# Loads four blocks ahead in a graph kernel's gate stage, dense rows two groups ahead in its mean stage

## The chip, the cores and the metric

One core of a Trainium2 chip. The metric is the device time of one execution in microseconds. A block below is 512 edges (4 tiles of 128); a node group is 1024 nodes. There are 98 of each.

## What is computed

Four graph layers over 100,000 nodes with 64 features and 50,000 edges sorted by destination: a mean of neighbours, a residual gated convolution (two gates), a four-head attention and a weighted SAGE layer, each followed by `x = layernorm(x + layer(x))`. What matters here is the end of the first layer, the dense half of the second layer that needs no edges, and the second layer's first gate:

```python
h = x + L0(x)                       # mean of neighbours, then layernorm -> x1
# first gate, per edge (src, dst), weights folded:
gate = sigmoid(k[dst] + q[src])     # k, q, v = x1 @ Wk1, x1 @ Wq1, x1 @ Wv1
agg  = segment_sum(gate * v[src], dst)
h1   = relu((agg + x1 @ Ws1 + b1) @ Wl1 + bl1)
# nodes without edges take the dense path: two matrix products, relu, add, layernorm
```

## The kernel before

The program is a row of stages; a barrier of all engines stands between two of them. Each stage writes an in-order program for each engine by hand; engines meet by counting semaphores alone. `over_pairs` calls a body `step(n, i, s, ...)` for every block, two to a loop iteration; `s = n % 2` picks one of two buffers. `ahead(n, i, s, k)` names block n+k, and `fresh(n)` is true where no earlier user of the buffer exists.

**Mean stage** (`spread_mean`, tag mb). GpSimd scatters the rows of runs (`x1_run`) into the table `x1_tab`: four indirect DMAs to a block (L1555), after indices that ScalarE copies (L1094). Beside it runs the dense path of node group n (`NodeStage`): SyncE loads `mb_xn` (L1533); TensorE transposes it (turn, L1131); ScalarE copies it (L1140); TensorE multiplies (hide, L1665); ScalarE takes the relu (L1619); TensorE multiplies again (multiply, L1149) into one PSUM bank; VectorE adds in four passes and a tiny one (`n_add`, L1573 to L1582); ScalarE squares (L1625); VectorE reduces (L1587); ScalarE takes the root (L1629, L1633); VectorE scales (`n_scale`, L1593); SyncE stores (L1159). A small edge MLP rides along, one half in even and the other in odd steps: in an odd step ScalarE runs z, abs, exp, ln (L1785 to L1793), VectorE `soft` (L1756), TensorE its second product (L1821). A load of rows n+2 waits until `n_add` of n has read its buffer (semaphore `n_used`, sent at L1577). In step n, ScalarE and TensorE turn and multiply group n+1, and VectorE reduces and scales n, then adds n+1.

**Gate stage** (`first_gate`, tag ga). Blocks go from last to first. For each: SyncE loads the block's own rows (`near`, L1860) and the flags that say which edges share a destination (`same`, 128 partitions, L1866); ScalarE copies the own rows into `ends` (put_near, L1975); GpSimd gathers the source rows with four indirect DMAs (L1102) after their indices (L1968); TensorE transposes (turn, L2026); ScalarE copies the lower half (L1989), VectorE scans the upper half by the flags (`spread_near`, L1915); TensorE forms the gates (produce, L2034); ScalarE takes the sigmoid (L1995); VectorE multiplies (L1922) and scans (`add_up`, L1931); TensorE mixes (L2042); VectorE finishes (L1939, L1944); SyncE stores (L1875). The order in step n is

```python
# SyncE:    load_near(n+2), load_same(n+2), store(n)
# ScalarE:  copy(n+2), locate(n+2), open_gate(n+2), index(n+4), put_near(n+4)
# TensorE:  mix(n), turn(n+2), produce(n+2)
# VectorE:  spread_near(n+2), weigh(n+1), add_up(n+1), finish(n)
# GpSimd:   rows_of(n+2)
```

`turn`, `spread_near`, `copy` and `produce` of a block reuse the buffers of the block two before: `spread_near(n)` waits for `mix(n-2)`, `rows_of(n)` for `turn(n-2)`.

Of the kernel before, what the change touches and what calls it, by code (L numbers as in the profile page):

```python
# [5 lines left out]
P = 128  # L6
D = 64
# [1494 lines left out]
def spread_mean(nc, a, st):  # L1502
# [3 lines left out]
    with Phase(nc, "mb") as ph:  # L1506
# [11 lines left out]
        node_turn, node_hidden, node_out = bank[0:3]  # L1518

        @block.sync  # L1520
        def _(sp):
            def load(n, i, s):
                if not fresh(n):
                    sp.wait_ge(scattered[s], 64 * i)
                    hold(sp, ph.passed)
                sp.dma_start(flat(run[s][:]), st["x1_run"][bass.ds(n * P, P)]).then_inc(run_in[s], 16)

            def load_x(n, i, s):
                if not fresh(n):
                    sp.wait_ge(node.turned, n - 1)  # L1530
                    sp.wait_ge(n_used, n - 1)
                    hold(sp, ph.passed)
                sp.dma_start(flat(xn[s][:]), table_rows(st["x1_node"], first_node(st, n))).then_inc(x_in[s], 16)  # L1533

            def step(n, i, s, first, last):
                if there(n + 2, BLOCKS):
                    load_x(*ahead(n, i, s, 2))
                    load(*ahead(n, i, s, 2))
                node.store(sp, st["attn_x"], n, i, s)

            for s in (0, 1):
                load(s, 0, s)
                load_x(s, 0, s)
            mlp.load(sp)
            over_pairs(sp, BLOCKS, step)
            node.all_stored(sp)
# [18 lines left out]
        def _(dve):  # L1565
            steps_n = Steps(dve, n_chain, 2)

            def n_add(n, i, s):
# [4 lines left out]
                nc.vector.tensor_tensor(node.v[s][:], product_rows(node_out), over_rows(rows[:, st["B_MIX2"], :]),  # L1573
# [22 lines left out]
            def step(n, i, s, first, last):  # L1596
                n_reduce(n)
                mlp.vector_before(dve, i, s, first)
                mlp.vector(dve, i, s, first)
                n_scale(n, i, s)  # L1600
                if there(n + 1, BLOCKS):
                    n_add(*ahead(n, i, s, 1))

            n_add(0, 0, 0)
            over_pairs(dve, BLOCKS, step)
            mlp.last_keep(dve)

        @block.scalar
        def _(act):
# [41 lines left out]
            node.copy(act, 0, node_turn)  # L1651
            n_relu(0)
            n_squares(0, 0, 0)
            over_pairs(act, BLOCKS, step)

        @block.tensor
        def _(pe):
# [10 lines left out]
            def n_multiply(n):  # L1668
                node.multiply(pe, n, node_out, st["w_pair"][2][:], h_t, softened)

            def step(n, i, s, first, last):
                more = there(n + 1, BLOCKS)
                if more:
                    n_turn(*ahead(n, i, s, 1))
                mlp.tensor_before(pe, i, s, first)
                if more:
                    n_hide(n + 1)
                mlp.tensor_after(pe, i, s, first)
                if more:
                    n_multiply(n + 1)  # L1680

            n_turn(0, 0, 0)
            n_hide(0)
            n_multiply(0)
# [144 lines left out]
def first_gate(nc, st):  # L1829
# [3 lines left out]
    with Phase(nc, "ga") as ph:  # L1833
# [11 lines left out]
        gathered, near_in, same_in, stored = ([ph.sem(f"{n}{s}") for s in (0, 1)] for n in (  # L1845
            "gathered", "near_in", "same_in", "stored"))
# [8 lines left out]
        def _(sp):  # L1855
# [13 lines left out]
            def step(n, i, s, first, last):  # L1869
                if there(n + 2, BLOCKS):  # L1870
                    load_near(*ahead(n, i, s, 2))
                    load_same(*ahead(n, i, s, 2))
# [4 lines left out]
            for s in (0, 1):  # L1877
                load_near(s, 0, s)
                load_same(s, 0, s)
            over_pairs(sp, BLOCKS, step)  # L1880
# [22 lines left out]
        def _(dve):  # L1903
            steps = Steps(dve, chain, 1)

            def spread_near(n, i, s):

                dve.wait_ge(turned, n + 1)
                dve.wait_ge(same_in[s], 16 * (i + 1))
# [15 lines left out]
            def add_up(n, i, s):  # L1925

                dve.wait_ge(paid, n + 1)
                if not fresh(n, 1):
                    dve.wait_ge(carried, n)
# [34 lines left out]
        def _(act):  # L1964
# [50 lines left out]
            over_pairs(act, BLOCKS, step)  # L2015

        @block.tensor
        def _(pe):
# [1643 lines left out]
```

## Time and profile before

| | us |
|---|---|
| median of 3 executions | 11201.8 (11200.99 to 11210.53) |
| the profiled execution: its time | 11221.07 |
| its span (first to last instruction) | 11219.4 |
| mean stage, in that span | 2447.7 to 3593.5 |
| gate stage | 3593.5 to 4928 |
| busy over the span: TensorE, VectorE, ScalarE, GpSimd | 49%, 58%, 39%, 61% |

The profile is of one execution. Times in its rows count from the start of the span. A timeline row gives start, duration, engine, line and operation (several instructions merged, with "xcount"), output<-input, and in brackets how long the engine had been idle and what ended that. PE is TensorE's matmul, PEld its weight load, DVE VectorE, ACT ScalarE, POOL GpSimd, SPq SyncE's queue. PEclk is the TensorE clock granted, as a share of full speed.

### The profile page before, as it was taken

How to read it: one execution, taken by the hardware profiler on the slowest of the kernel's cores; microseconds unless marked ns; L12 is line 12 of the kernel's file. 1: busy time of each engine (PE TensorE's matmuls, PEld its weight loads, DVE VectorE, ACT ScalarE, POOL GpSimd, SP SyncE). 2: the span in 40 equal slices, each digit the busy share in tenths (PEclk: the TensorE clock that was granted, in tenths of full speed). 3: DMA queues.
4: the chain of work that ended last, by engine and by line, in shares of the span. 5: the costliest groups of instructions: out<-in, count | busy, mean ns of one | idle time of the engine just before them, and what ended most of it. 6: DMA issues, size and time to landing. Idle time of an engine off the chain costs nothing. (4 is left out here: it accounts for less than half of the span.)

```text
span 11219.4 us, 129468 instructions
## 1 busy us (share of the span) xinstructions
PE 5525.8 (49%) x23165; PEld 4503.1 (40%) x23165; DVE 6495.9 (58%) x15506; ACT 4356.2 (39%) x11357; POOL 6848.6 (61%) x6784
## 2 busy tenths in 40 slices
PE   4210056655554333335555677677666666663222
PEld 1000055543333222223334666666666655553222
DVE  6767655544443333347776666666699974443333
ACT  1668644433332111137774333333355543331111
POOL 1767577753333222247777777777655557777777
PEclk6555577765555566655555555555566656665555
DMA  3000044441222111122221111111133334443222
GB/s 121 8 21 7 22 145 149 151 123 62 65 67 62 48 48 49 48 57 68 71 71 38 27 27 27 27 27 27 52 98 99 99 99 137 135 135 87 61 61 51
DMA packets 589304, 780.08 MB, mean 70 GB/s; under 512 B 153140, under 2 KB 306811, under 8 KB 585819
## 3 DMA queue, kind: packets, MB, share of 16 engines
q1 hardware_dynamic: 388540, 599.31, 16.5%
q0 software_dynamic: 200704, 180.15, 7.8%
q8 instruction: 17, 0.28, 0.0%
q14 instruction: 43, 0.34, 0.0%
HBM read 468.37 MB, written 322.23 MB: 70 GB/s over the span
## 5 line engine op out<-in xcount | busy, mean ns | idle before, releaser
L2603 DVE CUSTOM_DVE_ANT_0 att_junk<-bank,att_away 128x512 f32<-128x512 f32 x1568 | 973.5, 686 | 120.0 <-PE bank L2766 105.3
L1102 POOL DMA_INDIRECT ga_ends<-x_tab,ga_src_i x392 | 382.1, 975 | 950.7 <-ACT ga_src_i L1968 854.6
L1555 POOL DMA_INDIRECT x_tab<-mb_run,mb_put_i x392 | 389.9, 995 | 735.2 <-ACT mb_put_i L1094 621.1
L1003 PE MATMUL bank<-att_payload,att_match 128*128 128x68 f32 x3136 | 620.8, 383 | 190.9 <-DVE att_payload L2619 96.4
L1003 PEld LDWEIGHTS bank<-att_payload,att_match 128*128 128x128 f32 x3136 | 609.6, 298 | 221.5 <-issue 221.5
L2034 PE MATMUL bank<-ga_ends_t,w_gate 128*128 128x512 f32 x196 | 202.3, 1135 | 890.3 <-ACT ga_ends_t L1989 890.3
L1915 DVE TENSOR_TENSOR_SCAN ga_ends_t<-ga_same,ga_ends_t,bank 64x512 f32<-64x512 f32 x97 | 123.4, 1272 | 853.7 <-PE bank L2026 853.7
L471 POOL DMA_INDIRECT half_sorted<-ka_out_row,ka_put_i x392 | 397.1, 1013 | 286.6 <-ACT ka_put_i L604 172.1
L1102 POOL DMA_INDIRECT gb_ends<-h_tab,gb_src_i x392 | 432.0, 1102 | 150.1 <-issue 118.5
L674 POOL DMA_INDIRECT edges<-kb_out_row,kb_put_i x392 | 423.3, 1080 | 154.2 <-issue 121.9
L1102 POOL DMA_INDIRECT sa_ends<-x_tab,sa_dst_i x392 | 398.2, 1016 | 153.6 <-issue 135.5
L1102 POOL DMA_INDIRECT att_ends<-attn_x,att_dst_i x392 | 397.6, 1014 | 131.3 <-issue 102.1
L3605 PE MATMUL bank<-ident,sb_pay 128*65 128x128 f32 x392 | 109.5, 434 | 747.1 <-DVE sb_pay L3492 747.1
L1102 POOL DMA_INDIRECT ma_ends<-in_x,ma_src_i x392 | 376.6, 961 | 158.8 <-issue 130.8
L3460 POOL DMA_INDIRECT out<-sb_out,sb_put_i x392 | 397.6, 1014 | 121.7 <-issue 119.3
L2554 POOL DMA_INDIRECT attn_tab<-att_new,att_put_i x392 | 386.7, 986 | 135.9 <-issue 124.7
L1102 POOL DMA_INDIRECT sb_ends<-h_tab,sb_src_i x392 | 379.4, 968 | 137.6 <-issue 118.9
L2130 POOL DMA_INDIRECT attn_x<-gb_out,gb_put_i x392 | 387.6, 989 | 123.1 <-issue 105.2
L1102 POOL DMA_INDIRECT sa_ends<-x_tab,sa_src_i x392 | 379.4, 968 | 119.4 <-issue 110.6
L1102 POOL DMA_INDIRECT att_state<-attn_tab,att_row_i x392 | 370.4, 945 | 123.0 <-issue 123.0
L1102 POOL DMA_INDIRECT ma_ends<-in_x,ma_dst_i x392 | 370.2, 945 | 119.5 <-issue 111.2
L1102 POOL DMA_INDIRECT att_ends<-attn_x,att_src_i x392 | 370.0, 944 | 119.5 <-issue 116.1
(515 smaller groups left out, 20349.6 us busy)
## 6 DMA issues: line engine op xcount, KB each, us to landing
da_agg<-attn_tab SPq DMA_DIRECT2D x98, 288.0 KB, 2.9
attn_tab<-ka_attn_start SPq DMA_DIRECT2D x24, 1152.0 KB, 29.7
x_tab<-ma_wide SPq DMA_DIRECT2D x98, 260.0 KB, 2.0
ma_xn<-in_x SPq DMA_DIRECT2D x98, 256.0 KB, 3.4
x_node<-ma_n_out SPq DMA_DIRECT2D x98, 256.0 KB, 2.1
h_tab<-ma_n_out SPq DMA_DIRECT2D x98, 256.0 KB, 2.1
mb_xn<-x_node SPq DMA_DIRECT2D x98, 256.0 KB
attn_x<-mb_n_out SPq DMA_DIRECT2D x98, 256.0 KB, 2.1
```

The source lines that it names most:

```text
L471: nc.gpsimd.indirect_dma_start(st["half_sorted"], bass.IndirectOffsetOnAxis(ap=put_i[s][:, q:q + 1], axis=0), out_row[s][:, q, :], None).t ...
L674: nc.gpsimd.indirect_dma_start(st["edges"], bass.IndirectOffsetOnAxis(ap=put_i[s][:, q:q + 1], axis=0), out_row[s][:, q, :], None).then_in ...
L1003: ins = self.nc.tensor.matmul(bank[:, u * w:(u + 1) * w], self.match[s][:, t, u * P:(u + 1) * P], self.payload[s][:, t, :], start=(t == 0) ...
L1102: nc.gpsimd.indirect_dma_start(dst, None, table, bass.IndirectOffsetOnAxis(ap=index[:, q:q + 1], axis=0)).then_inc(sem, 16)
L1555: nc.gpsimd.indirect_dma_start(st["x1_tab"], bass.IndirectOffsetOnAxis(ap=put_i[s][:, q:q + 1], axis=0), run[s][:, q, :], None, bounds_che ...
L1915: nc.vector.tensor_tensor_scan(ends_t[s][0:D, ::-1], same[s][0:D, ::-1], turn_b[s][0:D, ::-1], before, ALU.mult, ALU.add).then_inc(spread, 1)
L2034: nc.tensor.matmul(gate_b[s][:], st["w_gate"][0][:], ends_t[s][:], start=True, stop=True).then_inc(produced, 1)
L2130: nc.gpsimd.indirect_dma_start(st["attn_x"], bass.IndirectOffsetOnAxis(ap=put_i[s][:, q:q + 1], axis=0), out[s][:, q, :], None, bounds_che ...
L2554: nc.gpsimd.indirect_dma_start(st["attn_tab"], bass.IndirectOffsetOnAxis(ap=put_i[s][:, q:q + 1], axis=0), new[s][:, q, :], None, bounds_c ...
L2603: ins = nc.vector.tensor_tensor_reduce(junk[h % 2][:, q, :], logit_t[h % 2][:], away[s][:, q, :], 1.0, -2.0 * BIG, ALU.subtract, ALU.max, ...
L3460: nc.gpsimd.indirect_dma_start(dest, bass.IndirectOffsetOnAxis(ap=put_i[s][:, q:q + 1], axis=0), out[s][:, q, :], None, bounds_check=N - 1 ...
L3605: ins = nc.tensor.transpose(turn_b[s][0:K, q * P:(q + 1) * P], pay[s][:, q, :], ident[:])
```

## The change

Mean stage: every part of the dense path moves one step earlier than VectorE: turn, hide and multiply of group n+2 run in step n; the last product alternates between two PSUM banks; VectorE scales group n-1, adds n+1, reduces n; ScalarE takes the root of n-1; SyncE stores n-1 after its loads. Gate stage: SyncE loads own rows of block n+4 in step n; the flags load is split into its upper half (64 partitions, for `spread_near`, block n+4) and its lower half (for `add_up`, block n+2), with a semaphore each; the store is that of n-1; TensorE's order is mix(n), produce(n+2), turn(n+3).

```diff
@@ spread_mean, sync
                     load_x(*ahead(n, i, s, 2))
                     load(*ahead(n, i, s, 2))
-                node.store(sp, st["attn_x"], n, i, s)
+                if not fresh(n, 1):
+                    node.store(sp, st["attn_x"], n - 1, i + s - 1, 1 - s)
@@ vector
             def step(n, i, s, first, last):
-                n_reduce(n)
                 mlp.vector_before(dve, i, s, first)
                 mlp.vector(dve, i, s, first)
-                n_scale(n, i, s)
+                if not fresh(n, 1):
+                    n_scale(n - 1, i + s - 1, 1 - s)
                 if there(n + 1, BLOCKS):
                     n_add(*ahead(n, i, s, 1))
+                n_reduce(n)
@@ scalar
-                more = there(n + 1, BLOCKS)
-                if more:
-                    node.copy(act, n + 1, node_turn)
-                n_root(n)
-                if more:
-                    n_relu(n + 1)
-                if there(n + 2, BLOCKS):
+                further = there(n + 2, BLOCKS)
+                if not fresh(n, 1):
+                    n_root(n - 1)
+                if further:
+                    node.copy(act, n + 2, node_turn)
                     index(*ahead(n, i, s, 2))
                 mlp.scalar(act, i, s, first)
-                if more:
+                if further:
+                    n_relu(n + 2)
+                if there(n + 1, BLOCKS):
                     n_squares(*ahead(n, i, s, 1))
@@ tensor
-            def n_multiply(n):
-                node.multiply(pe, n, node_out, st["w_pair"][2][:], h_t, softened)
+            def n_multiply(n, s):
+                pe.wait_ge(softened, n + 1)
+                if not fresh(n):
+                    pe.wait_ge(node.added, n - 1)
+                for r in range(4):
+                    ins = nc.tensor.matmul(node_out[s][:, r * P:(r + 1) * P], h_t[:, r * P:(r + 1) * P],
+                                           st["w_pair"][2][:], start=True, stop=True)
+                ins.then_inc(node.done, 1)
+
+            def step(n, i, s, first, last):
+                further = there(n + 2, BLOCKS)
+                if further:
+                    n_turn(*ahead(n, i, s, 2))
                 mlp.tensor_before(pe, i, s, first)
+                if further:
+                    n_hide(n + 2)
                 mlp.tensor_after(pe, i, s, first)
+                if further:
+                    n_multiply(n + 2, s)
...
@@ first_gate, sync
+            def load_near_same(n, i, s):
+                if not fresh(n):
+                    sp.wait_ge(spread, n - 1)
+                    hold(sp, ph.passed)
+                sp.dma_start(same[s][0:D, :], st["same_next"][bass.ds(back(n), 1)].broadcast_to([D, BLOCK])
+                             ).then_inc(near_same_in[s], 16)
...
-                sp.dma_start(same[s][:], st["same_next"][bass.ds(back(n), 1)].broadcast_to([P, BLOCK])
+                sp.dma_start(same[s][D:P, :], st["same_next"][bass.ds(back(n), 1)].broadcast_to([D, BLOCK])
                              ).then_inc(same_in[s], 16)
...
+            def step(n, i, s, first, last):
+                if there(n + 4, BLOCKS):
+                    load_near(*ahead(n, i, s, 4))
+                if there(n + 2, BLOCKS):
+                    load_same(*ahead(n, i, s, 2))
+                if there(n + 4, BLOCKS):
+                    load_near_same(*ahead(n, i, s, 4))
+                if not fresh(n, 1):
+                    store(n - 1, i + s - 1, 1 - s)
...
@@ tensor
                 mix(n, i, s)
                 if there(n + 2, BLOCKS):
-                    turn(*ahead(n, i, s, 2))
                     produce(*ahead(n, i, s, 2))
+                if there(n + 3, BLOCKS):
+                    turn(*ahead(n, i, s, 3))
 
             turn(0, 0, 0)
             turn(1, 0, 1)
             produce(0, 0, 0)
+            turn(2, 1, 0)
             produce(1, 0, 1)
```

Four blocks of own rows and flags are loaded ahead of the loop, and two node groups are turned and multiplied ahead of the loop of the mean stage.

## Rows read from the trace of the kernel before

**Rows 1.** Windows: length, busy us (x) of PE, PEld, DVE, ACT, POOL; PEclk, DMA share, GB/s

```profile
3000.00:3300.00 300.00, 151.19 (x481) 102.26 (x481) 122.34 (x220) 91.37 (x247) 103.08 (x104) 0.57 0.21 66
...
4200.00:4500.00 300.00, 94.12 (x308) 66.19 (x308) 93.41 (x132) 44.27 (x110) 86.42 (x88) 0.63 0.19 48
...
7000.00:7500.00 500.00, 352.57 (x1584) 324.09 (x1584) 348.76 (x1133) 182.81 (x471) 380.13 (x394) 0.58 0.13 27
```

**Rows 2.** Waits, 3650 to 4850 us: total us, times, longest

```profile
ACT ga_ends L1975 <- DMA ga_near<-x_run: 850.0, 88, 10.0
```

**Rows 3.** Timeline of the gate stage, two blocks

```profile
4200.99 0.42 ACT L1975 ACTIVATE ga_ends<-ga_near 128x256 f32<-128x256 f32 x1 [9.56 <-DMA ga_near<-x_run]
...
4202.09 2.08 PE L2034 MATMUL bank<-ga_ends_t,w_gate 128*128 128x512 f32 x2 [9.33 <-ACT ga_ends_t L1989]
...
4204.81 0.20 ACT L1968 ACTIVATE ga_src_i<-src_g 128x4 int32 x1
...
4206.42 1.27 DVE L1915 TENSOR_TENSOR_SCAN ga_ends_t<-ga_same,ga_ends_t,bank 64x512 f32<-64x512 f32 x1 [8.54 <-PE bank L2026]
...
4209.67 0.94 POOL L1102 DMA_INDIRECT ga_ends<-x_tab,ga_src_i  x1 [0.30 <-issue]
...
4210.74 0.43 DVE L1944 SCALAR_TENSOR_TENSOR ga_out<-ga_v,is_head 128x256 f32<-128x256 f32 x1 [0.37 <-DVE ga_v L1939]
4211.48 0.36 SPq L1875 DMA_DIRECT2D h_tab<-ga_out  x1
4212.59 0.34 SPq L1860 DMA_DIRECT2D ga_near<-x_run  x1
...
4214.72 0.42 ACT L1975 ACTIVATE ga_ends<-ga_near 128x256 f32<-128x256 f32 x1 [9.70 <-DMA ga_near<-x_run]
...
4228.30 0.42 ACT L1975 ACTIVATE ga_ends<-ga_near 128x256 f32<-128x256 f32 x1 [9.57 <-DMA ga_near<-x_run]
```

**Rows 4.** Tile view of ga_ends: the gathers' time from issue to landing

```profile
DMA to landing us min/median/max: 2.3/2.5/4.1
```

**Rows 5.** Timeline of the second gate: turn and mix back to back

```profile
5309.84 1.08 PE L2312 MATMUL bank<-ident,gb_ends 128*128 128x128 f32 x4 [5.86 <-DMA gb_ends<-h_tab,gb_src_i]
...
5310.72 1.80 PE L2329 MATMUL bank<-w_mix,gb_ends_t 128*128 128x64 f32 x8
```

**Rows 6.** Timeline of the mean stage, one pair of steps

```profile
3004.98 0.69 DVE L1577 SCALAR_TENSOR_TENSOR mb_n_v<-mb_n_v,mb_xn 128x512 f32<-128x512 f32 x1
...
3005.91 0.33 SPq L1533 DMA_DIRECT2D mb_xn<-x_node  x1
...
3011.35 0.20 ACT L1094 ACTIVATE mb_put_i<-tail_put 128x4 int32 x1
...
3013.87 0.68 DVE L1593 TENSOR_TENSOR mb_n_out<-mb_n_v,mb_rstd 128x512 f32<-128x512 f32 x1
3014.01 0.93 PEld L1821 LDWEIGHTS bank<-mb_mlp_w,mb_mlp_soft 128*128 128x128 f32 x4 [4.86 <-DVE mb_mlp_soft L1756]
...
3015.03 1.91 PE L1149 MATMUL bank<-w_pair,mb_h_t 128*128 128x128 f32 x8
...
3016.74 1.06 PE L1131 MATMUL bank<-ident,mb_xn 128*128 128x128 f32 x4
...
3028.99 0.33 SPq L1533 DMA_DIRECT2D mb_xn<-x_node  x1
```

**Rows 7.** Timeline of the mean stage's start

```profile
2448.10 0.43 SPq L1533 DMA_DIRECT2D mb_xn<-x_node  x1
...
2450.85 1.09 PE L1131 MATMUL bank<-ident,mb_xn 128*128 128x128 f32 x4 [9.06 <-DMA mb_xn<-x_node]
...
2452.62 2.08 PE L1665 MATMUL bank<-mb_n_rows_t,w_pair 128*128 128x512 f32 x2 [0.69 <-ACT mb_n_rows_t L1140]
```

**Rows 8.** Tile view of mb_put_i: the scatters' time from issue to landing

```profile
DMA to landing us min/median/max: 2.1/2.2/14.0
```

**Rows 9.** Timeline of the gate stage's start: one gate product

```profile
3610.48 1.12 PE L2034 MATMUL bank<-ga_ends_t,w_gate 128*128 128x512 f32 x2 [1.83 <-ACT ga_ends_t L1989]
```

More of the change, by code:

```diff
@@ L1517, in spread_mean @@
         block = ph.ctx.enter_context(nc.Block())
-        node_turn, node_hidden, node_out = bank[0:3]
+        node_turn, node_hidden, node_out = bank[0], bank[1], bank[2:4]
         @block.sync
@@ L1545, in _ @@
             over_pairs(sp, BLOCKS, step)
+            node.store(sp, st["attn_x"], BLOCKS - 1, BLOCKS // 2 - 1, 1)
             node.all_stored(sp)
@@ L1572, in n_add @@
                     dve.wait_ge(node.finished, n - 1)
-                nc.vector.tensor_tensor(node.v[s][:], product_rows(node_out), over_rows(rows[:, st["B_MIX2"], :]),
+                nc.vector.tensor_tensor(node.v[s][:], product_rows(node_out[s]), over_rows(rows[:, st["B_MIX2"], :]),
                                         ALU.add).then_inc(node.added, 1)
@@ L1650, in _ @@
                 index(s, 0, s)
-            node.copy(act, 0, node_turn)
-            n_relu(0)
+            for s in (0, 1):
+                node.copy(act, s, node_turn)
+                n_relu(s)
             n_squares(0, 0, 0)
             over_pairs(act, BLOCKS, step)
+            n_root(BLOCKS - 1)
         @block.tensor
@@ L1666, in n_hide @@
                                  ).then_inc(hidden, 1)
-            def n_multiply(n):
-                node.multiply(pe, n, node_out, st["w_pair"][2][:], h_t, softened)
+            def n_multiply(n, s):
[6 more added lines that the diff above has]
+                ins.then_inc(node.done, 1)
             def step(n, i, s, first, last):
-                more = there(n + 1, BLOCKS)
-                if more:
-                    n_turn(*ahead(n, i, s, 1))
+                further = there(n + 2, BLOCKS)
+                if further:
+                    n_turn(*ahead(n, i, s, 2))
                 mlp.tensor_before(pe, i, s, first)
-                if more:
-                    n_hide(n + 1)
+                if further:
+                    n_hide(n + 2)
                 mlp.tensor_after(pe, i, s, first)
[L1679 to L1684, printed above, removed]
+                if further:
+                    n_multiply(n + 2, s)
+            for s in (0, 1):
+                n_turn(s, 0, s)
+                n_hide(s)
+                n_multiply(s, s)
             over_pairs(pe, BLOCKS, step)
@@ L1844, in first_gate @@
                           "finished chain")
-        gathered, near_in, same_in, stored = ([ph.sem(f"{n}{s}") for s in (0, 1)] for n in (
-            "gathered", "near_in", "same_in", "stored"))
+        gathered, near_in, near_same_in, same_in, stored = ([ph.sem(f"{n}{s}") for s in (0, 1)] for n in (
+            "gathered", "near_in", "near_same_in", "same_in", "stored"))
         block = ph.ctx.enter_context(nc.Block())
@@ L1865, in load_same, with store @@
                     hold(sp, ph.passed)
-                sp.dma_start(same[s][:], st["same_next"][bass.ds(back(n), 1)].broadcast_to([P, BLOCK])
+                sp.dma_start(same[s][D:P, :], st["same_next"][bass.ds(back(n), 1)].broadcast_to([D, BLOCK])
                              ).then_inc(same_in[s], 16)
[L1869 to L1872, printed above, removed]
+            def store(n, i, s):
                 sp.wait_ge(finished, n + 1)
@@ L1875, in step @@
                 sp.dma_start(run_rows(st["h1_tab"], back(n)), flat(out[s][:])).then_inc(stored[s], 16)
[L1877 to L1880, printed above, removed]
+            def step(n, i, s, first, last):
[7 more added lines that the diff above has]
+                    store(n - 1, i + s - 1, 1 - s)
+            for n in range(4):
+                load_near(n, n // 2, n % 2)
+                load_near_same(n, n // 2, n % 2)
+                if n < 2:
+                    load_same(n, 0, n)
+            over_pairs(sp, BLOCKS, step, tail=6)
+            store(BLOCKS - 1, BLOCKS // 2 - 1, 1)
             for s in (0, 1):
@@ L1908, in spread_near @@
                 dve.wait_ge(turned, n + 1)
-                dve.wait_ge(same_in[s], 16 * (i + 1))
+                dve.wait_ge(near_same_in[s], 16 * (i + 1))
                 if not fresh(n, 1):
@@ L1927, in add_up @@
                 dve.wait_ge(paid, n + 1)
+                dve.wait_ge(same_in[s], 16 * (i + 1))
                 if not fresh(n, 1):
@@ L2014, in _ @@
                 put_near(s + 2, 1, s)
-            over_pairs(act, BLOCKS, step)
+            over_pairs(act, BLOCKS, step, tail=6)
         @block.tensor
```

1 line of the change is left out of this document (added).

## The prediction, made before the changed kernel was run

> **What bounds the kernel now.** The engines' shares of the whole span say little, since a dozen stages with different limits stand in a row; the change touches two. I read first the windows view by stage [rows 1]: in the mean stage the busiest engine, TensorE, works 151.19 of 300 us, in the gate stage 94.12 of 300 (VectorE 93.41, GpSimd 86.42). No engine is full and the DMA engines are at 0.19 to 0.21, so both stages are bound by a ring of waits, not by work. Two stages of 1146 and 1334 us hold what can be won.
>
> **Gate stage.** The waits view names the ring: ScalarE waits 850.0 us for the own rows (`near`) in 88 blocks [rows 2]. The timeline shows it once round [rows 3]. VectorE's finish of block n ends at 4211.17; SyncE first stores, and only then issues the load of block n+3 (4212.59); the rows are there at 4214.72; put_near stands ahead of `copy(n+2)` in ScalarE's queue, so the gate product, the mix and the turn all wait behind it. From 4200.99 to 4228.30 are two blocks: **13.66 us a block**.
>
> **Mean stage.** The load of node rows n+2 is issued when n_add has read its buffer (4.98 + 0.69, issue at 3005.91), and turn, copy, hide, relu, multiply and add of a group follow each other almost within one step. One load to the one two steps later takes 28.99 − 5.91 = **23.08 us a pair of steps** [rows 6], 11.54 a step.
>
> **The change in the gate stage.** Removed: the near load from that ring. In step n it now loads n+4. In SyncE's queue it stands behind the upper flags of n+3 (which wait for the scan of n+1) and behind the store of n−2; both are released at least one block before ScalarE wants the rows in step n, and a load takes 2.13 us (4212.59 to 4214.72), so it is covered by more than half a block. Its cost on the path is 0 and it would cost up to its 2.13 a block if that cover went. Added: one more DMA on SyncE. The queue has four a block instead of three; a store and the issue behind it take 4212.59 − 4211.17 = 1.42 together with the wake-up, so four take under 5.7 us even at that price each, less than the period below. The lower flags wait for `add_up(n)`; behind them stand the upper flags and the store, which only VectorE's finish of two blocks on and the next stage want. Cost 0; without that cover 1.42 a block.
>
> What is late next is the gather. Its indices still stand behind the sigmoid of `open_gate(n+2)`, and so behind the product of n+2, and `turn(n+4)` now comes just behind the product of n+3. Between two products of the same buffer, produce(n+2) and produce(n+4), lie these steps in series:
>
> - product end (2.09 + 2.08 = 4204.17) to the index copy at 4204.81: 0.64
> - index to the issue of the fourth gather, 4204.81 to 4209.67: 4.86 [rows 3]
> - issue to landing: 2.5 [rows 4]
> - turn(n+4) and mix(n+2) back to back, 5309.84 to 5312.52: 2.7 with the first weight load [rows 5]
> - spread_near(n+4), which may not start before mix(n+2) has read its buffer: 1.27 and about 0.04 to start
> - the product: 2.08 and 0.05
>
> The sum is 14.14 for two blocks, **7.07 a block**. The rings beside it are shorter. One block of TensorE alone (turn and mix 2.7, scan 1.31, product 2.13) is 6.14. GpSimd's four issues are (4209.67 − 4204.81) + 0.94, under 5.8. On VectorE scan, product, second scan and finish run from 4206.42 to 4211.17, that is 4.75. The gain is 13.66 − 7.07 = 6.59 a block. I count it for 94 of 98 blocks (the first sets up, the last three already have no loads to wait for): 619 us. Against it stands the start, where `turn(2)` is now queued ahead of `produce(1)` and must wait for the third gather: by the steps above the first finish comes some 5 us later, an estimate. **Net −614.**
>
> The bounds: the landing can be 2.3 to 4.1 [rows 4]. At 4.1 for every block the ring is 15.7, or 7.9 a block; with TensorE at the higher clock (below) it is 6.1.
>
> **The change in the mean stage.** Nothing is added but a second PSUM bank. The moves take the reduce, root and scale of n and the product of n+1 off the series path, since VectorE adds n+1 from a product made one step earlier. What is left in series over two steps, from the index copy of an odd step, is [rows 6, 7]:
>
> - index, z, abs, exp, ln, soft and scale, 3011.35 to 3014.55: 3.20
> - two passes of n_add until the buffer is free: twice 0.69 and gaps, 1.52
> - SyncE's issue after that, 3005.67 to 3005.91: 0.24
> - the load: 2.75 (2448.10 to 2450.85, the same load with three others beside it)
> - turn 1.09, copy until the next product starts 0.68, hide 2.08
> - the MLP's first product and multiply; the like pair runs from 3014.01 to 3016.94: 2.93
> - the next turn up to 3017.80: 0.86; its copy until the index: 0.55
>
> The sum is **15.9 a pair**. VectorE's and ScalarE's ring is shorter: an even step is three full passes and a reduce more (each 0.69), a root and a scale, some 5.6, and an odd one has the 3.2 of the MLP on top, about 14.5 together. The stores now stand behind the loads in SyncE's queue; the load in the sum waits for `n_used`, which comes after `finished` of the group before, so that queueing costs 0. The scatters have 15.9 us for their eight issues, which take 8 × 1.28 (the 0.97 to 1.0 of one and 0.3 between) = 10.2; cover enough. The gain is 23.08 − 15.9 = 7.18 a pair, for 47 of 49 pairs: **−337**. The load is the term I know least: no row shows its landing in the middle of the stage. It lies between 2.1 (a like load of half the size in the gate stage) and, if it meets the scatters, about the gathers' longest 4.1; that is −0.65 to +1.35 a pair.
>
> **The sum.** 614 + 337 = 951 us off the profiled execution's 11221.07 gives 10270. That execution was 19.3 us above the median of the runs, so on the median's scale I forecast **10251**.
>
> **Where a rule and the rows part.** At 3610.48 one gate product took 1.12 us, at 4202.09 it took 2.08 [rows 3, 9]: the higher and the lower of TensorE's two levels, 2.4 and 1.2 GHz. TensorE today rests 9.33 us ahead of each gate product; after the change its longest rest in a block is about 1.4. I keep 2.08, because in the stage at 7000 us TensorE is busy 352.57 of 500 us, as densely as the changed gate stage would be (4.8 of 7.07), and is granted 0.58 [rows 1].
> The Trainium skill (TensorE: Matmul & The Clock Gate, "HAM oscillation") speaks the other way: long idle gaps are what sends the clock back, so closing them should keep it released. By that rule the sum would be that of rival A; the row at 7000 does not agree with it.
>
> **Rivals.**
> *A, the clock stays up* (chance 0.08). A product saves 0.96, the mix and turn together about 0.9 by the same ratio: 1.9 in the gate ring, 6.1 a block, 90 us more. In the mean stage hide, the product pair and two turns save some 2.6 a pair, 122 more. The time is 10040. For it: the short gaps. Against: 0.58 at 7000.
> *B, transfers collide* (0.14). At half the period the same bytes give DMA shares of 0.3 to 0.4, in bursts, and every gather and load lands late: gathers at 4.1, 0.8 a block more, 78 us; the node load at 4.1, 63 us more; and some 40 more (an estimate) where GpSimd issues each gather slower. The time is about 10430.
> *C, own rows or another SyncE wait still end last in the gate stage* (0.05), because SyncE's queue has four waits in order. Then only the mean stage gains: 11202 − 337 = 10865. Against it speaks that every wait in that queue is satisfied a block early.
> *D, slower* (0.03): broadcast loads clog the DMA engines. At the start of the mean stage, where eight small broadcast loads go out, a scatter took 14.0 us to land instead of 2.2 [rows 8]. The flags are such loads, and there are now two to a block. If each gather landed after 14.0, the gate ring would be 14.14 + 11.5 = 25.6, or 12.8 a block, 81 us faster than today; if the node load in the mean stage, which now ends last there, took 14 too, its pair would be 15.9 − 2.75 + 14 = 27.2, 192 us slower. The time would be 11202 + 111 = 11313. It turns at a landing of about 13 us in both. Against it: today's flags land without delaying a gather, 2.5 in the median.
> The Trainium skill (DMA: Bandwidth & Descriptors, "Rules for kernel authors") says two transfers to disjoint partition halves serialize and are not worth issuing; no row here shows a split flags load. Both halves have a block or more of slack, so this alone only feeds D.
>
> **How the numbers follow.** My forecast has 0.70. Its own range: the gate ring 6.9 to 8.0 a block, the mean pair 14.9 to 18, gives 10160 to 10440. The range that holds 8 in 10 is a little wider, 10130 to 10460: A and C to D stay out, B is in. Same means within 0.2% (22 us), about what a measurement of this kernel can tell; a landing just there needs a mix of C and D: 0.02. Faster 0.95, slower 0.03.
>
> **What would show it.** In the changed profile: the gate stage about 720 us long; the wait of put_near for `ga_near` gone, and in its place TensorE's turn waiting for the gathers and VectorE's scan waiting for the mix; GpSimd waiting for the index copy about 2 us a block; blocks in pairs of about 6.1 and 7.9 us. In the mean stage a pair of steps of 15.9, with TensorE waiting about 2.4 us in even steps for `mb_xn`, and no wait of VectorE for L1149's product. Products of 2.08 say the clock stayed; 1.12 says A. All other stages keep their lengths. The forecast is wrong if the gate block is over 8 us, or if a pair of the mean stage stays above 18.

## The result and the profile after

The changed kernel takes **10282.77 us** in the median (10278.6 to 10287.13, 4 runs) against 11202.19 of the kernel before beside it: ratio 0.9178 [0.9162, 0.9194]. The prediction was 10251, with 10130 to 10460. Below, a stage's length is the time from its first load to the next stage's first load, in the profiled execution.

| us | before | after | predicted step |
|---|---|---|---|
| mean stage | 1145.8 | 784.9 (−361) | −337 |
| gate stage | 1334.4 | 780.2 (−554) | −614 |
| second gate (code unchanged) | 1080.8 | 1063.2 | 0 |
| profiled execution | 11221.07 | 10278.6 (−942.5) | −951 |

The windows view of the kernel after, one row in the mean stage and one in the gate stage (length; busy us of PE, PEld, DVE, ACT, POOL; PEclk; DMA share; GB/s), answers [rows 1]:

```profile
2500.00:3200.00 700.00, 417.71 (x1654) 283.15 (x1653) 422.48 (x763) 311.33 (x855) 374.97 (x359) 0.78 0.31 97
3300.00:3950.00 650.00, 364.99 (x1176) 250.20 (x1176) 356.37 (x503) 159.81 (x420) 326.52 (x336) 0.55 0.35 85
```

No engine is full in either stage (60% at most): rings of waits still set the time, only shorter ones. TensorE's granted clock rose from 0.57 to 0.78 in the mean stage; in the gate stage it went from 0.63 to 0.55 [rows 1]. Such a mean also covers the time in which TensorE rests: the gate products themselves took 2.0 us or more in nearly every block before, and 1.10 in 22 of 98 after.

**Gate stage.** The waits view after, 3350 to 3900 us, about 71 blocks (waiting instruction, releaser, total us, times, longest):

```profile
DVE ga_ends_t L1945 <- PE bank L2073: 205.2, 71, 5.4
ACT ga_gate L2026 <- PE bank L2065: 170.1, 69, 2.7
...
POOL ga_ends L1102 <- PE bank L2057: 149.0, 29, 5.9
PE bank L2057 <- DMA ga_ends<-x_tab,ga_src_i: 128.0, 36, 5.1
...
POOL ga_ends L1102 <- ACT ga_src_i L1999: 52.3, 33, 4.9
```

The 850 us of [rows 2] are gone (put_near waits 4.2 us in the whole stage). In their place stand the waits that the prediction named: the scan for the mix, the turn for the gathers, GpSimd for the indices. (The view puts 149.0 us of GpSimd's waits down to a turn, L2057. By the program the gathers wait only for the turn of two blocks before, which is long done then; the turn named ends within 0.01 us of the index copy, 3602.35 + 1.06 and 3603.21 + 0.20, so the index copy is the release.) The timeline of the kernel after follows the ring once round (start, duration, engine, line, operation):

```profile
3600.51 2.04 PE L2065 MATMUL bank<-ga_ends_t,w_gate 128*128 128x512 f32 x2 [1.51 <-ACT ga_ends_t L2020]
...
3603.21 0.20 ACT L1999 ACTIVATE ga_src_i<-src_g 128x4 int32 x1
...
3606.07 1.10 PE L2065 MATMUL bank<-ga_ends_t,w_gate 128*128 128x512 f32 x2 [1.41 <-ACT ga_ends_t L2020]
...
3607.86 0.34 SPq L1873 DMA_DIRECT2D ga_near<-x_run  x1
...
3608.07 0.94 POOL L1102 DMA_INDIRECT ga_ends<-x_tab,ga_src_i  x1 [0.30 <-ACT ga_src_i L1999]
...
3608.54 0.50 SPq L1886 DMA_DIRECT2D ga_same<-same_next  x1
...
3611.53 1.09 PE L2057 MATMUL bank<-ident,ga_ends 128*128 128x128 f32 x4 [4.37 <-DMA ga_ends<-x_tab,ga_src_i]
...
3612.41 1.80 PE L2073 MATMUL bank<-w_mix,ga_ends_t 128*128 128x64 f32 x8
...
3614.35 1.27 DVE L1945 TENSOR_TENSOR_SCAN ga_ends_t<-ga_same,ga_ends_t,bank 64x512 f32<-64x512 f32 x1 [4.67 <-PE bank L2073]
...
3615.72 2.04 PE L2065 MATMUL bank<-ga_ends_t,w_gate 128*128 128x512 f32 x2 [1.51 <-ACT ga_ends_t L2020]
```

Product end to index 0.66 (3602.55 to 3603.21), index to fourth issue 4.86, issue to turn 3.46, turn to mix end 2.68, scan and wake-up 1.51, product 2.04: 15.21 for two blocks, against 14.14 in the prediction. The blocks come as 5.56 and 9.65. Over the stage a pair takes 15.47 (90 loads of L1873, so 89 blocks, from 3276.5 to 3964.9); in the pairs on either side of the one shown the last gather is used 3.73 and 3.74 after its issue (3592.59 to 3596.32 and 3623.27 to 3627.01).

**Mean stage.** The waits view after, 2600 to 3200 us (39 pairs of steps), then a line of the same view before, 2600 to 3500 us, that has no counterpart after, and then the timeline of one pair after:

```profile
ACT mb_square L1629 <- DVE mb_var L1589: 206.1, 77, 4.7
...
DVE mb_mlp_soft L1769 <- ACT mb_mlp_e L1806: 176.8, 39, 5.0
...
PE bank L1131 <- DMA mb_xn<-x_node: 137.1, 48, 4.0
```

```profile
DVE mb_n_v L1573 <- PE bank L1149: 266.2, 78, 4.5
```

```profile
2811.95 0.33 SPq L1533 DMA_DIRECT2D mb_xn<-x_node  x1
...
2815.05 0.63 PE L1131 MATMUL bank<-ident,mb_xn 128*128 128x128 f32 x4 [3.91 <-DMA mb_xn<-x_node]
...
2816.44 2.07 PE L1671 MATMUL bank<-mb_n_rows_t,w_pair 128*128 128x512 f32 x2 [0.66 <-ACT mb_n_rows_t L1140]
...
2821.23 1.06 PE L1131 MATMUL bank<-ident,mb_xn 128*128 128x128 f32 x4
...
2822.82 0.20 ACT L1094 ACTIVATE mb_put_i<-tail_put 128x4 int32 x1
...
2822.98 1.13 PE L1671 MATMUL bank<-mb_n_rows_t,w_pair 128*128 128x512 f32 x2 [0.69 <-ACT mb_n_rows_t L1140]
...
2825.34 0.68 DVE L1595 TENSOR_TENSOR mb_n_out<-mb_n_v,mb_rstd 128x512 f32<-128x512 f32 x1
...
2826.96 0.69 DVE L1579 SCALAR_TENSOR_TENSOR mb_n_v<-mb_n_v,mb_xn 128x512 f32<-128x512 f32 x1
...
2827.89 0.33 SPq L1533 DMA_DIRECT2D mb_xn<-x_node  x1
```

From load to load 15.94 (23.08 in [rows 6]; predicted 15.9; over the stage a pair takes 15.6, by the loads at 2484.30 and 3202.27, 46 pairs apart): load to turn 3.10, turn and copy 1.39, hide to the end of the next turn 5.85, copy to index 0.53, index to the end of scale 3.20, two adds and the issue 1.87. TensorE waits for the load in about every even step, and VectorE no longer waits for the last product.

### The profile page after: what moved, and what is told of

Read it like the earlier page. It is cut to its first block and busy times, and to the rows that moved or that the text cites. A ratio compares the mean times of both kernels' runs of the same rounds, so it can differ in the third digit from the quotient of the medians.

```text
span 10276.9 us, 130260 instructions
## 1 busy us (share of the span) xinstructions
PE 5401.1 (53%) x23165; PEld 4394.1 (43%) x23165; DVE 6499.3 (63%) x15506; ACT 4347.1 (42%) x11357; POOL 6834.7 (67%) x6784
## 5 line engine op out<-in xcount | busy, mean ns | idle before, releaser
L1557 POOL DMA_INDIRECT x_tab<-mb_run,mb_put_i x392 | 410.8, 1048 | 358.2 <-ACT mb_put_i L1094 248.5
L2921 POOL TENSOR_TENSOR da_weighed<-da_v,rows 128x512 f32<-128x512 f32 x98 | 124.6, 1271 | 414.7 <-DVE da_v L2985 414.7
L3638 PEld LDWEIGHTS bank<-ident,sb_pay 128*65 128x65 f32 x392 | 70.5, 220 | 766.3 <-DVE sb_pay L3525 766.3
```

Of the source, the lines that this page charges most:

```text
L1557: nc.gpsimd.indirect_dma_start(st["x1_tab"], bass.IndirectOffsetOnAxis(ap=put_i[s][:, q:q + 1], axis=0), run[s][:, q, :], None, bounds_che ...
L2921: nc.gpsimd.tensor_tensor(weighed[s][:], v[s][:], over_rows(rows[:, st["B_LNG"], :]), ALU.mult).then_inc(weighing, 1)
L3638: ins = nc.tensor.transpose(turn_b[s][0:K, q * P:(q + 1) * P], pay[s][:, q, :], ident[:])
```

## The experiments

The first eight runs (`mean_only` to `store_only`, then `no_flags` to `store_index`) were made on one chip, where the kernel before took 11217.36 (first four) and 11206.28 us (next four). `no_loads` and the three with early indices at the end came last. These last four ran on **another chip, where the kernel before took 12811.52 us** (12796.39 to 12842.88). There they are compared with each other and by ratio; against the first chip only with the caution that the second gate, unchanged, takes 1325 to 1327 us there instead of 1063 to 1086. The traces show where: there ScalarE waits 217.3 us in 47 waits (L1060, `no_loads`) for something that the profile calls "remote", of which the traces of the first chip show none. In the first gate's stage three of the four show no such wait either, and `turn_two_index_first` 14.4 us. The mean stage, the same code in all of them, takes 791 to 804 us there instead of 785. What "remote" stands for here is open.

### One stage alone

`mean_only` is the kernel before with the new `spread_mean`; `gate_only` the kernel before with the new `first_gate`.

> The change in the mean stage alone, the gate stage as before. Theory 1 (the two stages gain apart, their gains add): the mean stage takes 785 us as in the changed kernel, the gate stage 1334 as before, the time 11202 - 361 = about 10840. Rival (some of the gate's gain comes from what the mean stage leaves behind, such as a warmer clock or warmer queues, or the reverse): mean stage over 800 us, or a gate stage that is not 1334, and gains that do not add up to 919.

> The change in the gate stage alone. Theory 1: mean stage 1146 us, gate stage 780, the time about 11202 - 555 = 10647. Rival: as for the run before it. If theory 1 holds, the two gains add to 919 within 15 us.

Measured: 10850.81 (0.9676 [0.966, 0.9692]) and 10643.25 (0.949 [0.9475, 0.9506]); the mean stage 782.9 in the one, the gate stage 777.8 in the other, as in the whole. The gains of 3.24% and 5.10% make 8.34% against 8.22% together, which is within the intervals. (In us it is 941 against 919, more than the 15 allowed for beforehand; the kernel before was itself 15 us slower in this round.) With the stages' lengths this makes the two halves independent, and each may be explained by itself. The waits of `gate_only` are those of the whole (the turn for the gathers 144.0 us in 43 times from 3700 to 4300).

### Indices ahead of the sigmoid

```diff
@@ first_gate, scalar, step (and likewise ahead of the loop)
                     locate(*ahead(n, i, s, 2))
+                    if there(n + 4, BLOCKS):
+                        index(*ahead(n, i, s, 4))
                     open_gate(*ahead(n, i, s, 2))
                 if there(n + 4, BLOCKS):
-                    index(*ahead(n, i, s, 4))
                     put_near(*ahead(n, i, s, 4))
```

> The changed kernel, but ScalarE copies the gather's indices of block n+4 before the sigmoid of n+2, so that the gathers no longer wait for the product. Theory 1 (the gate ring is product, sigmoid, index, four gathers and their landing, turn, mix, scan, product: 15.2 to 15.5 us for two blocks): the ring breaks there and what is left is TensorE's own ring of turn, mix, scan and product, 6.1 to 6.5 us a block; gate stage 620 to 660 us instead of 780, time 10140 to 10170. Rival 2 (the scan's wait for the mix, or GpSimd's own issue rate with a store and four loads beside it, is what ends last): gate stage within 20 us of 780, time 10260 to 10290.

Measured: **10094.37** (0.9001 [0.8986, 0.9016]), gate stage 586.0: faster than expected, and the best version of all. Timeline of this run, and one line of its waits view (3350 to 3850 us, 77 blocks):

```profile
3600.00 0.19 ACT L1999 ACTIVATE ga_src_i<-src_g 128x4 int32 x1
...
3600.65 2.05 PE L2066 MATMUL bank<-ga_ends_t,w_gate 128*128 128x512 f32 x2 [1.41 <-ACT ga_ends_t L2020]
...
3605.07 0.94 POOL L1102 DMA_INDIRECT ga_ends<-x_tab,ga_src_i  x1 [0.30 <-issue]
...
3606.66 2.04 PE L2066 MATMUL bank<-ga_ends_t,w_gate 128*128 128x512 f32 x2 [1.51 <-ACT ga_ends_t L2020]
...
3608.49 1.06 PE L2058 MATMUL bank<-ident,ga_ends 128*128 128x128 f32 x4
```

```profile
PE bank L2058 <- DMA ga_ends<-x_tab,ga_src_i: 19.6, 26, 3.4
```

The index is copied before the product starts instead of 0.66 after its end, 3.4 us sooner (2.05 + 0.66 + 0.65), and the fourth gather goes out 3.4 us ahead of its turn. This turn does not wait, and all turns together wait 19.6 us for gathers in 77 blocks, where they waited 128.0 in 71. The period is 6.01 and then 5.90 (next product 3612.56): even blocks, and close to TensorE's own ring of 6.14 that the prediction summed. So the ring through indices and gathers is what sets the changed gate stage.

### Which part of the gate change pays

`store_only` has the new mean stage and of the gate change only this:

```diff
@@ first_gate (before), sync, step
                     load_same(*ahead(n, i, s, 2))
-                sp.wait_ge(finished, n + 1)
...
+                if not fresh(n, 1):
+                    store(n - 1, i + s - 1, 1 - s)
```

> Mean stage as changed; in the gate stage the kernel before with one edit alone: SyncE stores block n-1 instead of n, behind the loads. No load further ahead, no split flags, the turn two ahead. Theory 1: the ring of before was closed by the near load behind the store; with the store out of its way the near load is early, and the ring through the whole flags load (add_up(n), load 3.4 us, scan(n+2), multiply, add_up(n+1)) of 7.0 to 7.6 us a block is next, gate stage 700 to 760 us, time 10200 to 10265, at least as fast as the whole change. Rival 3 (the four-ahead loads are what wins): gate stage near 1334 or at least over 900, time over 10400.

Measured: 10277.59 (0.9162 [0.9147, 0.9178]), gate stage 755.1, as expected. One edit is worth as much as the whole gate change. Its waits, 3350 to 3850 us:

```profile
ACT ga_ends L1993 <- DMA ga_near<-x_run: 222.2, 66, 4.9
...
POOL ga_ends L1102 <- ACT ga_src_i L1986: 172.8, 64, 4.0
...
DVE ga_ends_t L1933 <- DMA ga_same<-same_next: 61.0, 29, 2.4
```

Own rows still end last, but 3.4 us a time instead of 9.7. `store_index` adds the early indices to it (same edit as above):

> Mean stage as changed; gate stage of the kernel before with two edits: SyncE stores n-1 behind the loads, and ScalarE copies the indices of n+4 before the sigmoid of n+2. No further-ahead loads, no split, turn two ahead. Theory 1: with the gather ring broken the flags ring (add_up(n), load, scan(n+2), multiply, add_up(n+1)) of 7.0 to 7.6 us a block stays, gate stage 700 to 750 us, time 10215 to 10265; so the split and the four-ahead loads are worth 110 to 160 us once the indices are early (gate stage 586 with them). Rival 7 (they are worth nothing even then): gate stage 580 to 620, time 10085 to 10120.

Measured: 10226.01 (0.9124 [0.9108, 0.9139]), gate stage 718.3, as expected, and put_near still waits 217.8 us for its rows. Together with the runs above:

| gate stage, us | indices late | indices early |
|---|---|---|
| store one step later only | 755.1 | 718.3 |
| whole change | 780.2 | 586.0 |

The loads four ahead and the turn three ahead lose 25 us as long as the indices are late, and win 132 once they are early.

### The gathers' late landing

The one term that missed is issue to landing, 3.46 instead of 2.5. Own rows and upper flags go out within 0.5 us of the fourth gather (3607.86 and 3608.54 beside 3608.07). `no_flags` leaves out all loads of flags after the second block; `unsplit` is the changed kernel with the flags loaded in one piece, two ahead:

```diff
@@ no_flags, sync
-                    load_same(*ahead(n, i, s, 2))
...
-                    load_near_same(*ahead(n, i, s, 4))
@@ unsplit, sync and vector
-                if there(n + 4, BLOCKS):
-                    load_near_same(*ahead(n, i, s, 4))
...
-                sp.dma_start(same[s][D:P, :], ...broadcast_to([D, BLOCK])
+                sp.dma_start(same[s][:], ...broadcast_to([P, BLOCK])
...
-                dve.wait_ge(near_same_in[s], 16 * (i + 1))
+                dve.wait_ge(same_in[s], 16 * (i + 1))
```

> The changed kernel without the flags loads after the first two blocks (the scans read old flags; 128 kB twice a block less on the DMA engines and two issues less on SyncE). In the changed kernel the gathers of one pair landed 3.4 and 3.7 us after the issue of the last of four, 2.5 before. Theory 1 (other transfers stretch the landing, and the landing sits in the ring): it falls back towards 2.5 to 2.9, a pair of blocks to 14.2 to 14.7 us, the gate stage from 780 to 715 to 745, the time to 10215 to 10245. Rival 4 (the late landing comes from the gathers themselves, eight of which now follow each other closely): gate stage 770 to 785, time 10270 to 10285.

> The changed kernel with the flags in one load of 128 partitions again, two blocks ahead. Theory 1: the scan of n+2 then waits for a load that starts only after add_up(n); a ring of 7.0 to 7.6 us a block through that load stands beside the gather ring of 7.7 and holds up one block of each pair by up to 1.6 us: gate stage 790 to 860 us, time 10290 to 10365. Rival 5 (splitting into partition halves buys nothing, one DMA less on SyncE helps): gate stage 760 to 782, time 10260 to 10285.

`no_flags`: 10267.5 (0.916 [0.9145, 0.9175]), gate stage 751.2, 29 us less than the whole and between the two theories. Timeline of `no_flags`:

```profile
3590.37 0.34 SPq L1873 DMA_DIRECT2D ga_near<-x_run  x1
...
3593.43 0.94 POOL L1102 DMA_INDIRECT ga_ends<-x_tab,ga_src_i  x1 [0.30 <-issue]
...
3596.17 1.08 PE L2053 MATMUL bank<-ident,ga_ends 128*128 128x128 f32 x4 [3.54 <-DMA ga_ends<-x_tab,ga_src_i]
3596.40 0.34 SPq L1873 DMA_DIRECT2D ga_near<-x_run  x1
```

The gather is used 2.74 after its issue. SyncE's queue being shorter, the own rows too have moved away from it, so this run does not tell what flags and own rows do apart. Its pairs take 14.65, 14.49 and 15.26 (products at 3571.22, 3585.87, 3600.36 and 3615.62), the long one with a gather that took 1.65 us to issue instead of 0.94.

`unsplit`: 10256.21 (0.9149 [0.9133, 0.9164]), gate stage 743.4. My theory (790 to 860) was wrong and the rival's direction right, though the gain is larger than its 760 to 782. Timeline of `unsplit`:

```profile
3604.53 0.94 POOL L1102 DMA_INDIRECT ga_ends<-x_tab,ga_src_i  x1 [0.30 <-issue]
3604.54 2.04 PE L2062 MATMUL bank<-ga_ends_t,w_gate 128*128 128x512 f32 x2 [1.51 <-ACT ga_ends_t L2017]
...
3606.86 0.33 SPq L1886 DMA_DIRECT2D ga_same<-same_next  x1
3607.21 1.08 PE L2054 MATMUL bank<-ident,ga_ends 128*128 128x128 f32 x4 [0.63 <-DMA ga_ends<-x_tab,ga_src_i]
...
3611.55 2.05 PE L2062 MATMUL bank<-ga_ends_t,w_gate 128*128 128x512 f32 x2 [1.65 <-issue]
```

The gather is there 2.68 after its issue, no load went out within 2 us of it, and the blocks are nearly even (7.01, and 7.49 up to the product at 3619.04). Splitting the flags costs the changed kernel 37 us of stage, although the scan of `unsplit` waits for them at times. The Trainium skill (DMA: Bandwidth & Descriptors, "Rules for kernel authors") advises against two transfers to disjoint partition halves; here the run agrees, by those 37 us. Slow issues play a part beside the landing: 21 of the gathers of `no_flags` took over 1.5 us to issue, 2 of those of `unsplit`, which may be why `unsplit` is the faster of the two.

`no_loads` leaves out the loads of own rows and of flags after the second block (the other chip):

> The changed kernel without own-row and flags loads after the first two blocks of the gate stage (old rows and flags are used); the gathers and the store are what is left on the DMA engines. Theory 1 (gather ring as summed in the prediction, 14.14 us a pair with a landing of 2.5; what the changed kernel takes beyond that, 15.3 us a pair, is other transfers beside the last gather): 14.1 to 14.4 us a pair, gate stage 705 to 725 us against 780 whole and 751 without flags, time 10210 to 10235. Rival 4 (the gathers hold up each other): gate stage 745 us or more.

Measured: 11874.23 (0.9264 [0.9249, 0.928]), gate stage 747.6. The timeline of `no_loads`, two pairs:

```profile
3984.48 2.04 PE L2059 MATMUL bank<-ga_ends_t,w_gate 128*128 128x512 f32 x2 [1.51 <-issue]
...
3998.91 2.04 PE L2059 MATMUL bank<-ga_ends_t,w_gate 128*128 128x512 f32 x2 [1.51 <-issue]
...
4005.21 1.82 POOL L1102 DMA_INDIRECT ga_ends<-x_tab,ga_src_i  x1 [0.30 <-issue]
...
4007.33 0.94 POOL L1102 DMA_INDIRECT ga_ends<-x_tab,ga_src_i  x1 [0.30 <-issue]
...
4010.07 1.09 PE L2051 MATMUL bank<-ident,ga_ends 128*128 128x128 f32 x4 [4.64 <-DMA ga_ends<-x_tab,ga_src_i]
```

With no load beside it the last gather lands in 2.74, and a pair takes 14.43 (3984.48 to 3998.91): the sum of the prediction, 14.14, with a landing 0.2 and other terms 0.1 longer. The next pair takes 15.35 (product at 4014.26), by a gather of 1.82 us to issue; one comes in about every third pair, in `no_flags` too, which is 0.3 a pair. So the loads beside the gathers do stretch the landing, by some 0.7 us in the pair shown and 1.0 in its neighbours (rival B's mechanism), and a part of what their removal gives goes into slower issues. At 747.6 the run ended above its 705 to 725 and within the rival's "745 or more"; but the rival's mechanism is not there, since the gathers follow each other as closely as ever and land in 2.74. As the run was on the other chip, how much of the excess is the chip's stays open, and so does why every third pair has such a gather.

### What the early indices need beside them

All three have the early indices, on the other chip. No run there has the early indices and nothing else changed, so `turn_two_index_first` has to serve for comparison. `index_unsplit` loads the flags in one piece, `index_near_two` the own rows two ahead again, `turn_two_index_first` has TensorE's old order.

```diff
@@ index_near_two, sync, step
-                if there(n + 4, BLOCKS):
-                    load_near(*ahead(n, i, s, 4))
+                if there(n + 2, BLOCKS):
+                    load_near(*ahead(n, i, s, 2))
@@ turn_two_index_first, tensor, step
                 if there(n + 2, BLOCKS):
+                    turn(*ahead(n, i, s, 2))
                     produce(*ahead(n, i, s, 2))
-                if there(n + 3, BLOCKS):
-                    turn(*ahead(n, i, s, 3))
```

> Indices early (gate stage 586 us with the rest of the change), flags unsplit in one load two ahead. Theory 1: the ring add_up(n), SyncE and the flags load (3.3), scan(n+2) 1.3, multiply 0.7, add_up(n+1) 1.3 gives 7.0 us a block, gate stage 690 to 725 us, time 10195 to 10230; the split is then worth over 100 us, though in the changed kernel itself it cost some. Rival 5 (the split is never worth anything): gate stage 580 to 600.

> Indices early, flags split, but own rows loaded two blocks ahead. Theory 1: finish(n), store, load 2.2, put_near(n+4), copy(n+3), product 2.1, turn and mix 2.7, scan, multiply, scan, finish(n+2) make a ring of some 13.8 us for two blocks, gate stage 660 to 700 us, time 10165 to 10205; loading own rows four ahead is then worth about 90 us. Rival 8 (moving the store alone was what freed the own rows): gate stage 580 to 600, time 10085 to 10110.

> Indices early and all loads as in the change, but TensorE's old order: mix(n), turn(n+2), produce(n+2). Theory 1: TensorE's ring of mix, turn, scan and product is as long in either order, 5.9 to 6.2 us a block, gate stage 580 to 620 us, time 10085 to 10125. Rival 9 (turning three ahead carries the gain): gate stage over 650.

| run | us | ratio | gate stage |
|---|---|---|---|
| index_unsplit | 11858.83 | 0.9252 [0.9236, 0.9268] | 723.4 |
| index_near_two | 12232.23 | 0.9546 [0.953, 0.9562] | 1091.5 |
| turn_two_index_first | 11781.22 | 0.9193 [0.9178, 0.9208] | 656.9 |

`index_unsplit`, waits from 3800 to 4200 us:

```profile
DVE ga_ends_t L1942 <- DMA ga_same<-same_next: 130.2, 55, 2.7
```

The 723.4 us are within the expected 690 to 725. The scan waits 2.4 us a block for flags that could not be loaded before add_up of two blocks earlier. This is what the split is for: it costs 37 us with late indices, and with early ones the run with it is 66 us shorter (656.9 in `turn_two_index_first`, which also has TensorE's old order, so the 66 are not the split's alone). Here the rule of the Trainium skill (DMA: Bandwidth & Descriptors, "Rules for kernel authors") does not hold: the two halves have different readers, and it is the wait for the later one that the split removes.

`index_near_two` was expected at 660 to 700: the direction was right and the size far off. Its waits from 3800 to 4200 us, ScalarE's and then SyncE's queue's:

```profile
ACT ga_ends L2007 <- DMA ga_near<-x_run: 264.6, 36, 8.2
```

```profile
SPq L46 <- DVE ga_ends_t L1946: 274.0, 35, 8.4
```

The load of own rows n+4 now stands behind the upper flags of n+5 in SyncE's order, and those wait for the scan of n+3. But put_near(n+4) stands ahead of `copy(n+3)` and everything of block n+3 behind it on ScalarE. Once the flags are asked for four ahead, own rows two ahead sit behind them, in a ring of 11 us a block. I had not followed that queue.

`turn_two_index_first` came out above its 580 to 620, at 6.4 a block (products at 4001.38 and 4007.78, against 6.0 in `index_first`). At 656.9 it lies where its rival, that turning three ahead carries the gain, put it (over 650). The 14.4 us of "remote" waits do not explain the 71 us to `index_first`, but the two ran on different chips, so what the turn order is worth is not shown.

### Half of each node row

`half_rows` loads only half of each node row in the mean stage.

```diff
@@ spread_mean, sync, load_x
-                sp.dma_start(flat(xn[s][:]), ...)
+                cols = slice(0, 512 if fresh(n) else 256)
+                sp.dma_start(flat(xn[s][:])[:, cols], ...[:, cols])
```

> The changed kernel, but from the third node group on only half of each node row is loaded in the mean stage (the other half keeps old values; 128 kB instead of 256). Theory 1 (the node load closes the mean stage's ring, TensorE waits for it some 3 to 4 us in even steps): landing 0.5 to 0.8 us sooner, a pair of steps that much shorter, mean stage 745 to 765 instead of 785, time 10240 to 10260. Rival 6 (VectorE's and ScalarE's ring of add, reduce, root, scale ends last): mean stage 780 to 786, time within 6 us of 10283.

Measured: 10255.34 (0.9149 [0.9134, 0.9165]), mean stage 762.3. Timeline:

```profile
2812.62 0.33 SPq L1534 DMA_DIRECT2D mb_xn<-x_node  x1
...
2815.20 0.83 PE L1131 MATMUL bank<-ident,mb_xn 128*128 128x128 f32 x4 [3.38 <-DMA mb_xn<-x_node]
...
2828.15 0.33 SPq L1534 DMA_DIRECT2D mb_xn<-x_node  x1
```

The load lands 0.52 sooner (2.58 instead of 3.10), the pair is 0.41 shorter (15.53 instead of 15.94) and the stage 23 us, or 0.46 a pair: the node load does close the ring.

## Why the prediction came out right, step by step

The mechanism was right in both stages. The closeness of the total is in part luck: the gate stage gained 60 us less than forecast, and the mean stage 24 more and the second gate 17.6 without a known cause, so that on the profiled executions 942.5 us stand against the forecast's 951. On the medians the miss is 32 us, since the profiled execution before lay 19.3 above its median and the one after 4.2 below.

- **Own rows leave the gate ring**: shown; [rows 2] went from 850.0 us to 4.2. Rival C falls.
- **The gather ring sets the gate stage**: shown by `index_first`, which shortens that ring alone and takes 194 us off the stage. Five of its six terms are within 0.2 us.
- **The landing of 2.5** was the mis-sized term: 3.46 in the pair shown and 3.7 in its neighbours. The 2.5 was the median of all four gathers of a block, and that median is still 2.5 after; the ring holds the last one, with the loads beside it. The stage's 15.47 a pair instead of 14.14 is 0.66 a block; times 94 it makes 63 us, the 60 missing. It was inside the bounds (2.3 to 4.1), and is rival B at a small scale: it was named there as a case of its own, where the sum should have carried half of it.
- **"Added: one more DMA on SyncE ... Cost 0"** failed. I only asked whether the queue keeps up, not what the new transfer does to the gather beside it. It costs about 37 us (`unsplit`), and `no_flags` puts the flags as a whole at 29.
- **The mean ring** was right in nearly every term; the load took 3.10 instead of 2.75, and turn and copy 1.39 instead of 1.77, as one turn of each pair ran in 0.63 instead of 1.09. The pair shown is one of the longer ones: 15.6 over the stage, against 23.15 before (loads at 2486.43 and 3551.23, 46 pairs apart). That is 7.5 a pair instead of 7.18, and the forecast counted 47 of 49 pairs; together they cover the 24 us that the stage gained beyond it.
- **The other stages keep their lengths**: nearly. The second gate is 17.6 us shorter here, but in the eight runs of the first chip it takes 1074 to 1086 with the same code, so this is no effect of the change that a run shows.
- **The clock**: the forecast kept the lower level. In the mean stage the granted clock rose to 0.78 and hide took 1.13 in odd steps; in the gate stage it was 0.55, and the second product took 1.10 in about every other pair. So rival A came true in part and brought little: the faster gate product (3606.07) lies in the block of 5.56, which has slack. The prediction's "longest rest of about 1.4" was wrong, as a turn that waits for its gathers is itself a rest: 4.37 us once a pair in the gate stage (3611.53), 3.91 in the mean stage (2815.05). The Trainium skill (TensorE: Matmul & The Clock Gate, "HAM oscillation") would have the clock kept up once long gaps are closed. They were not closed, and the product that follows the long rest runs at the lower level (2.04 and 2.07), the one after it often at the higher (1.10 and 1.13), which agrees. `index_first` has rests of 1.4 to 1.5 in the blocks shown; it was still granted 0.59 (3300 to 3750 us), with about three products in ten at 1.10, which does not agree.
- **D, clogged DMA**: no sign. The longest gather takes 4.3 us to land, the longest flags load 3.5.

## What to carry to other kernels

When the longest wait of a stage is removed, sum the ring that remains and move its first link before the rest: here copying four indices ahead of a sigmoid was worth 188 us more (10094.37 against 10282.77), and the loads four ahead pay only with it (together with the turn three ahead, 25 us lost without it and 132 won with it). Price an added transfer by what is in flight beside it, not only by whether its queue keeps up. And try the smallest edit that breaks the ring first: with the new mean stage, the store moved by one step gave the whole gain of the gate change (`store_only`, 10277.59).

## What the runs showed of the hardware

- The same program took 11206 to 11217 us on one chip and 12811.52 on another, 14% more. A gate product takes 2.04 and a gather 0.94 to issue on both; the second gate is over 20% longer (1325 to 1327 against 1063 to 1086), nearly all of it in "remote" waits (217.3 us in `no_loads`), which the first chip's traces do not have.
- An indirect DMA, 0.94 to issue as a rule, takes 1.56 to 1.94 once in about every third pair of blocks with no flags or no loads in the stage (`no_loads`: 3960.97, 4005.21, 4049.60), and seldom in `unsplit` and `index_first` (twice and once).
- Within one stage the same product takes 2.04 in most blocks and 1.10 in about one of four (22 of 98), at a granted clock of 0.55 over the stage.
- The median time of all gathers from issue to landing stayed 2.5 us while the last of each four, with two loads beside it, took 3.46 to 3.74 up to its use: a median over a block's transfers hides the one that ends the ring.
